# One transformer layer on one core: attention unrolled, row maxima sent in halves, routing of the first batch placed in groups 4 to 7

## The reference

```python
x = x + attention(layernorm(x))      # x: 2 batches x 1024 tokens x 128, 16 heads of width 8
x = x + ffn(layernorm(x))            # 8 experts, top 2, capacity 512
# attention
q, k = rotary(x @ Wq + bq), rotary(x @ Wk + bk);  v = x @ Wv + bv
att = softmax(causal((q @ k.T + bias(bucket(i - j))) / sqrt(8)))
y = (att @ v) @ Wp + bp
# ffn, on u = layernorm(x)
probs = softmax(u @ Wr);  w, e = top_k(probs, 2)
pos = running count of the expert's earlier tokens;  keep = pos < 512
buf[e, pos] = u
buf_out = (gelu(rms(buf) @ Wg) * (rms(buf) @ Wu)) @ Wd + buf
combined = u + sum(w * buf_out[e, pos]);  fout = gated net of width 64 on rms(u), + u
out = where(a token overflowed, fout, combined)
```

## Time and profile before

| | us |
|---|---|
| median of 3 runs | 473.86 (473.33 to 474.39) |
| the profiled execution's own time | 474.48 |
| its span, first to last instruction | 472.7 |

### The profile page before, as it was taken

How to read it: one execution, slowest core, us unless ns; L and a number is a source line. 1 busy time by engine, 2 the same in 40 slices (tenths; PEclk the granted TensorE clock), 3 DMA queues, 4 the chain that set the end, 5 groups by cost and what they waited for, 6 DMA issues and landing times.

```text
span 472.7 us, 8283 instructions
## 1 busy us (share of the span) xinstructions
PE 384.9 (81%) x2440; PEld 184.7 (39%) x2440; DVE 320.9 (68%) x702; ACT 212.4 (45%) x471; POOL 283.7 (60%) x229
## 2 busy tenths in 40 slices
PE   3297398699999999997999999986877495999910
PEld 0154143343444434433434444342434241566510
DVE  3989369687786786864877867749566780466614
ACT  1024212377676776763766776766442100233300
POOL 6637800096767858863967669677367384066660
PEclk9689879799999999998999999998898597799975
DMA  8196881650532893507106200053001012123118
GB/s 231 34 272 135 174 185 23 162 99 2 95 78 79 269 183 64 112 6 133 39 3 122 50 3 1 0 164 105 2 23 55 27 46 67 47 85 96 46 44 266
DMA packets 32560, 42.90 MB, mean 91 GB/s; under 512 B 6043, under 2 KB 26395, under 8 KB 31147
## 3 DMA queue, kind: packets, MB, share of 16 engines
q1 hardware_dynamic: 29334, 35.62, 32.2%
q0 software_dynamic: 2048, 4.11, 2.6%
q10 hardware_dynamic: 1136, 2.65, 1.7%
HBM read 27.61 MB, written 12.75 MB: 85 GB/s over the span
## 4 chain that ended last, share of the span: by engine, by line
PE 63%; DVE 15%; DMA 7%; issue 7%; POOL 5%; SPq 1%; ACT 1%; ACTq 0%; DVEq 0%; POOLq 0%
PE ps_av L922 15%; PE ps_st L898 14%; PE ps_slot L826 13%; PE ps_slot L830 6%; PE ps_st L1017 3%; PE ps_slot L1027 3%; POOL slots L608 2%; DVE neg_max L1181 2%; DMA b_grp<-b_all 2%; PE ps_st L1019 2%; PE ps_slot L941 1%; PE ps_av L1019 1%; DMA bcol<-in_L_attn_bk_dram 1%; PE ps_slot L865 1%; POOL parts L617 1%
## 5 line engine op out<-in xcount | busy, mean ns | idle before, releaser
L1181 DVE TENSOR_REDUCE neg_max<-ps_slot 128x1 f32<-128x640 f32 (+7 forms) x184 | 176.1, 990 | 50.4 <-PE ps_slot L830 48.9
L688 ACT ACTIVATE probs<-ps_st 128x512 f32<-128x512 f32 (+3 forms) x384 | 164.6, 495 | 90.3 <-PE ps_st L898 88.0
L593 POOL TENSOR_TENSOR probs<-probs,f_grp 128x1024 f32<-128x1024 f32 (+1 forms) x70 | 140.9, 2018 | 5.3
L826 PE MATMUL ps_slot<-k_stack,q_stack 128*128 128x512 bf16 (+3 forms) x384 | 103.9, 336 | 10.4 <-DMA b_grp<-b_all 4.1
L898 PE MATMUL ps_st<-q_stack,k_stack 128*128 128x512 bf16 (+3 forms) x384 | 100.1, 332 | 4.7 <-DMA q_stack<-max_rows 3.2
L589 POOL TENSOR_SCALAR_AFFINE_SELECT probs<-probs 128x512 f32<-128x512 f32 x63 | 40.0, 635 | 100.1 <-ACT probs L688 100.0
L922 PE MATMUL ps_av<-probs,v_grp 128*32 128x512 f32 (+3 forms) x768 | 82.5, 504 | 0.7 <-POOL probs L593 0.4
L830 PE MATMUL ps_slot<-b_grp,flip_b 128*128 128x256 bf16 (+1 forms) x288 | 69.9, 267 | 0.0
L898 PEld LDWEIGHTS ps_st<-q_stack,k_stack 128*128 128x128 bf16 x384 | 34.9, 98 | 66.7 <-ACT probs L688 47.2
L826 PEld LDWEIGHTS ps_slot<-k_stack,q_stack 128*128 128x128 bf16 x384 | 36.5, 100 | 48.4 <-DVE neg_max L1181 14.5
L617 POOL DMA_INDIRECT parts<-probs,e_tok x32 | 31.4, 983 | 31.0 <-DVE probs L1433 22.2
(11 more groups left out here) (156 smaller groups left out, 391.3 us busy)
## 6 DMA issues: line engine op xcount, KB each, us to landing
q_stack<-q_parts SPq DMA_DIRECT2D x24, 192.0 KB
f_grp<-f_all SPq DMA_DIRECT2D x6, 512.0 KB, 10.1
slots<-in_c_rows_dram SPq DMA_DIRECT2D x4, 528.0 KB, 5.9
probs<-slots SPq DMA_DIRECT2D x8, 264.0 KB, 2.7
f_all<-g_vec SPq DMA_DIRECT2D x1, 2048.0 KB, 11.3
k_stack<-k_parts SPq DMA_DIRECT2D x16, 128.0 KB
b_grp<-b_all SPq DMA_DIRECT2D x8, 256.0 KB
parts<-in_c_rows_dram SPq DMA_DIRECT2D x4, 512.0 KB, 10.0
```

Of the source, the lines that this page charges most:

```text
L593: pool.tensor_tensor(pr, pr, f_grp[:, fbuf, :, fo:fo + hi - lo], ALU.mult).then_inc(near_done, 1)
L688: act.activation(probs[:, u % PBUF, g, c0:512], ps_st[:, n % 3, c0:512], ACT.Exp, scale=SCALE).then_inc(exp_done, 1)
L826: pe.matmul(ps_slot[:, slot, o + lo:o + hi], q_stack[:, buf, g, t * P:(t + 1) * P], k_stack[:, buf, g, lo:hi], start=True, stop=(nlo >= nhi))
L1181: dve.tensor_reduce(neg_max[:, heads[0]:heads[-1] + 1, t], src, AX.X, ALU.max, negate=True).then_inc(slot_used, 1)
```

## The change

- The loops and steps go. A list `PLAN`, made when the program is built, gives every item of all 8 groups in one order, and each engine walks it. The scores and values are laid out first; the maxima units of group n+1 are spread by their matmul columns from row 8 of group n to row 8 of group n+1 (a row is one ST; a group has 48). Group 0: 12 (with the one due at once, 13) maxima units ahead of its first ST, the rest with FLIPs 2 to 7 among its rows 0 to 7.
- Maxima in halves: M comes twice for a group, directly behind maxima unit 6 (queries 0 to 511) and behind unit 22. The scores of the second half of the queries (row 16 on) wait for the second M alone. `M_AT = 58` is now `M_AT = [6, 22]`.
- SP: `put_max(n, 0)`, `load_stack(n + 2)` (nine DMAs, once the exponentials of group n-1 are done), `put_max(n, 1)`. The stacks are stored by halves of the tokens; group 0's halves are loaded apart, the first after quarter 0.
- Quarters 0, 1, 2 are projected, then maxima units 0 to 6, M, then quarter 3, FLIP 0 and 1. DVE's statistics of batch 1 stand behind the rotation of quarter 1. `keep_warm(8)` stands behind quarter 2.
- `b_grp`, `f_grp` and `v_grp` and their copies go: PE and POOL read `b_all`, `f_all` and `v_all`. `VW`, the columns of a head's values, is 9 and not 32. `f_all` is loaded in two parts.
- Tokens: batch 0's units stand in groups 4 and 5 (A0 in unit 54, E0 in unit 67 of 96); POOL sends 12 of its 16 rows between its products from unit 70 on. Batch 1 is two spans of 4 tiles: A2, B2 in group 7, C2 and D1 among the last values, the second span behind. F and G stand last.

```diff
-SPANS = [(0, TPB), (TPB, TT)]
+SPANS = [(0, TPB), (TPB, TPB + CH), (TPB + CH, TT)]
+TOKENS_AT = {54: [("A", 0)], 55: [("A", 1)], 57: [("B", 0)], 59: [("B", 1)], 62: [("C", 0)], 63: [("C", 1)],
+             64: [("D", 0)], 65: [("X", 0)], 67: [("E", 0)], 92: [("A", 2)], 93: [("B", 2)], 94: [("NEAR", 10)],
+             95: [("NEAR", 11)]}
+TOKENS_LAST = [("A", 3), ("E", 1), ("B", 3), ("C", 3), ("D", 2), ("X", 2), ("E", 2),
+               ("F", 0), ("F", 1), ("F", 2), ("F", 3), ("G", 0), ("G", 1), ("G", 2), ("G", 3)]
...
+    out = [("QK", 0), ("QK", 1), ("QK", 2)]
+    d = 0
+    for i, (items, cost) in enumerate(t_items):
+        while d < len(due) and due[d][0] <= before[i]:
+            out.append(due[d][1])
+            if due[d][1] == ("M", 0, 0):
+                out += [("QK", 3), ("FLIP", 0), ("FLIP", 1)]
+            if due[d][1][0:2] == ("S", 0) and due[d][1][2] >= len(SUNITS) - N_FLIP + 2:
+                out.append(("FLIP", due[d][1][2] - len(SUNITS) + N_FLIP))
+            d += 1
         out += items
+    av = [("AV", NG - 1, u) for u in range(NU - AV_LAG, NU)]
+    return out + [av[0], ("C", 2), av[1], ("D", 1), av[2], ("EVAC", NG - 1, 1), ("X", 1), ("Y", NG - 1, 1)]
...
+                elif kind == "M":
+                    pe.wait_ge(slot_used, k)
+                    pe.transpose(ps_slot[0:HG * MT, slot, 0:P],
+                                 neg_max[:, what[2], :, :].rearrange("p g t -> p (g t)"), ident).then_inc(slot_full, 1)
...
+            for n in range(1, NG):
+                put_max(n, 0)
...
+                if n + 2 < NG:
+                    load_stack(n + 2)
+                put_max(n, 1)
...
+                    near_product(n, u)
+                    if NU * n + u >= DISPATCH_FROM and sent < 2 * TPB and (NU * n + u) % 3:
+                        if sent == 0:
+                            pool.wait_ge(init_out, 16 * E_NUM // 2)
+                        dispatch(*rows[sent])
+                        sent += 1
```

More of the change, by code:

```diff
@@ new lines, in t_cost, with s_cost, transposed_items @@
+def t_cost(u):
+    return HG * (512 - first_col(*UNITS[u]))
+def s_cost(su):
+    t, heads = SUNITS[su]
+    return len(heads) * (t + 1) * P
+def transposed_items():
+    out = []
+    for n in range(NG):
+        for u in range(NU):
+            tile, back = (u - AV_LAG) % NU, (1 if u < AV_LAG else 0)
+            items = [("ST", n, u, g) for g in range(HG)]
+            av = []
+            if n >= back:
+                av = [("AV", n - back, tile)]
+                if tile in (CH - 1, NU - 1):
+                    av.append(("EVAC", n - back, int(tile == NU - 1)))
+            at = AV_AT[u]
+            rows = [[i] for i in items]
+            if at < HG:
+                rows[at] = av + rows[at]
+            else:
+                rows[HG - 1] += av
+            if u == Y_AT[1] and n:
+                rows[HG - 1].append(("Y", n - 1, 1))
+            if u == Y_AT[0]:
+                rows[HG - 1].append(("Y", n, 0))
+            rows[HG - 1] += TOKENS_AT.get(NU * n + u, [])
+            out += [(r, t_cost(u) / HG) for r in rows]
+    return out
@@ new lines, in _, with stack_rows, part_rows @@
+            load_tiles(b_all, r_vec, 0, H, toep_in)
+            load_tiles(f_all, g_vec, 0, HG, factors_in)
+            def stack_rows(stack, buf, row, n, halves):
+                return stack[row:row + n, buf, halves[0]:halves[-1] + 1, :, :].rearrange("p h g t -> p h (g t)")
+            def part_rows(parts, n, part, count, halves):
+                w = HG * CW
+                return bass.AP(tensor=parts, offset=((n * NM + halves[0]) * 3 + part) * D * w,
+                               ap=[[w, count * D], [3 * D * w, len(halves)], [1, w]])
@@ L482, in _ @@
[L482 to L491 removed]
+            put_max(0, 1)
+            load_stack(2)
+            for n in range(1, NG):
+                put_max(n, 0)
+                if n + 2 == NG // 2:
+                    for i in range(2):
+                        for j in range(2):
+                            sp.wait_ge(parts_out[i][j], 2 * PART_OUT)
+                if n + 2 < NG:
+                    load_stack(n + 2)
+                put_max(n, 1)
+                if n == 2:
@@ new lines, in _ @@
+            sent = 0
+            for n in range(NG):
+                for u in NEAR:
+                    if n == NG - 1 and u in LAST_NEAR:
+                        continue
+                    near_product(n, u)
[4 more added lines that the diff above has]
+                        sent += 1
@@ L612, in _ @@
+            for t, k in rows[sent:]:
+                dispatch(t, k)
             pool.wait_ge(zero_out, 16 * (B * T // CAP))
@@ L646, in _, with split @@
             copy_xnT(0)
-            for c in range(NCH):
+            def split(c):
+                if c == 0:
+                    copy_xnT(1)
                 for i in range(2):
```

740 lines of the change are left out of this document (342 added, 398 removed).

## The result

The changed kernel takes 517.83 us (median of 4 runs, 517.32 to 523.16) beside 474.12 for the kernel before (473.33 to 476.5, 4 runs): ratio 1.0925, interval 1.0881 to 1.0968. Slower was right; 488 was 30 us short, and 517.8 lies outside the range (479 to 496) and above every rival's case.

The account below looks back on a forecast made before the run. PE was taken to bound the loop's steps, so its stalls are paid in full. Six terms gave 363.1 to the last exponential, + 30.5 + 23 + 70.3 = 486.9 us span, 488 on the median's footing; range 479 to 496.

Parts of the forecast that it names:

- E0: Batch 0's token unit in unit 67 of 96: ends the 36.6 us stretch of DVE's token work; no PE standing named.
- Term 1: Start: first maxima unit at 57 us, row 8 of group 0 reached at 90, bounds 83 and 93.
- Term 2: Seven stretches of scores with the next group's maxima: PE's work unchanged, 7 x 30.7 = 214.9 us.
- Term 3: M directly behind its last maxima unit, groups 1 to 7: PE stands still 14 x 1.54 = 21.6 us.
- first rival: PE's stalls at M are absorbed, so the 21.6 us go: 464 us, chance 0.20.
- Term 4: Second rows of maxima behind a stack's loads, groups 1 to 5: 0.4 us a group, 2 in all, bounds 0 and 24.
- third rival: Rows of maxima wait out the whole stack, 4.9 us late in five groups: 510 us, 498 if half; chance 0.12.
- Term 5: Batch 0's tokens in groups 4 and 5: DVE's excess work and waits cost 14 us, bounds 6 and 21.
- fourth rival: DVE's token work grows beside POOL, each norm piece doubling again: +7 us, 495 us, chance 0.09.
- Term 6: Group 7 and tail: ACT bounds scores, 20.6 us; then 30.5 to last positions, 23 to experts, 70.3 for experts.
- all cases: 464 to 498: Whole kernel: the time range stated for the forecast and all rivals together, in us.

Follow-up runs that it names:

- The experiment in the old kernel: Kernel before, with M directly behind the last maxima unit of a step and not 8 items later: 487.71 us, ratio 1.0286.
- the later M: Changed kernel with second rows of maxima ahead of the stack's loads and 14 of 16 M one maxima unit later: 494.47 us, ratio 1.0415.
- after_sp: Changed kernel with the second row of maxima issued on SP's queue ahead of a stack's nine loads: 506.93 us, ratio 1.0662.
- the fill: Changed kernel with 16 warm-up matmuls added behind token unit B1 and 8 behind each of D0 and E0: 512.85 us, ratio 1.0789.
- after_newton0: Changed kernel without the three Newton rounds in batch 0's second norm: 520.95 us, ratio 1.0661, on a chip where the kernel before took 488.0.
- the trace without rows: Changed kernel with none of POOL's token rows between its products, all 32 following the last product: 515.34 us, ratio 1.0846.
- best3: Changed kernel with maxima rows ahead of loads, M one unit later, 18 warm-up matmuls, norm in pieces, other batch 0 tokens in group 7, tail filled: 487.79, 472.56 us.

## Why the prediction fell short

By the prediction's terms, from the trace (the forecast span was 486.9, the measured 516.1):

- **Term 1, start.** Row 8 of group 0 stands at M(0, 1): 91.1 for 90. The total is right, in part by luck: the maxima started at 55.0 for 57, and from there it took 36 us and not 33.
- **Term 2, the stretches.** Too small by 0.8 a group, 5.6 us. Terms 2 and 3 made a plain group 33.8; it is 34.60 with two M a group, and PE is busy 31.50 in it and not 30.70. The row that grew is the turned scores' (13.3 us for 12.4); why was not separated. The narrower values gave half a microsecond a group at most (96 matmuls in 10.0 us, before 100 in 10.9). Group 0's stretch is 2.0 shorter than a plain one (32.6), which the prediction did not have: it holds 80 value matmuls and not 96.
- **Term 3, M behind its unit.** The mechanism is right, the size a little high. M's idle time is 1.32 for 1.54, in 14 places of groups 1 to 7 (one of them, 4.03, also holds D0's block), so 18.5 for 21.6. The experiment in the old kernel shows the wait alone (1.69 at each M), and the later M takes most of it away. The first rival (464) is refuted by both.
- **Term 4, rows behind the loads.** Mis-sized: 2 forecast; 7.6 on PE's rows and 10.3 in the traces. The step that failed is "behind the loads it lands with them, near 9.5 to 10". The rows take 6.4 to 7.4 us from issue, near the 8.64 of the earlier trace rows that I kept as the bound. "It decides from 5.0 us of landing time on" was right: 6.37 gives a wait of 1.36, 7.43 one of 2.43. It is the third rival's mechanism at less than half its size (22).
- **Term 5, tokens in groups 4 and 5.** The step that failed most: 14 forecast, 28.5 measured. The amount on DVE was right (69.5 busy in both groups, 21.1 over two plain ones, for 23.7). What was wrong is "25.6 + 23.7 - 36.6 = 12.7 too much" as the whole price: it lets DVE fill all its idle time, and nothing is added to it for PE. Shown in its place: DVE stays idle 28.3 of 97.7 us (`after_sp`), while PE stands behind each block and hands over nothing; the one block that was shortened went into the time whole (1.75 for 1.75). The standing is 15.0 in all. So the 14 would have been about right for the standing alone; what the term left out is the lower clock behind each standing (6.6, by the fill), for which the prediction had no figure, and PE's own token matmuls, about 7, which it had only as the lower bound. The places of the standings were named rightly (7.67 for "5 to 9", 4.03 for 3), and E0's 3.73 was left out. The fourth rival's mechanism is there (2.20 us at L1088, and the 4.69 of L1264 in `after_newton0`), but for 2 us here, not for the bulk.
- **Term 6, group 7 and the tail.** Group 7 took 26.9 for 20.6. The step that failed is "without maxima ACT bounds the scores". 1.9 are POOL's rows of tokens (25.0 without). For the other 4.4 no run changes one engine alone, but the trace without rows shows that ACT was not the bound: in 368.1 to 393.1 ACT is busy 17.8, POOL 19.9 and PE 21.9 us, so PE's own work was already more than 20.6, and the chain passes from one to the other. Behind it the forecast held: positions 28.2 us after the last exponential for 30.5, the experts 21.4 after that for 23, straight behind the warm-up; 69.5 for 70.3.

Summed: +1.1 (start), +5.6 (plain groups), -2.0 (group 0's stretch), +8.3 (rows of maxima), +14.5 (tokens), +6.3 (group 7), -4.7 (tail and experts) = 29.1 of the 29.2 that the span was off.

The range had a fault of its own: "all cases: 464 to 498" leaves out the 510 that the third rival is priced at, and each case changes one or two terms. Here terms 2, 4, 5 and 6 were all too low at once.

As for the change itself: with its three new waits mended the unrolled kernel reaches 472.6 to 475.5, level with the kernel before or 0.6% under it. Its plain group is then still 1.8 us longer than the old step (32.49 for 30.70), about 12.5 us over seven. So about as much must be gained elsewhere (no loop turn, earlier start, no copies, the shorter warm-up); what each of these gives was not measured alone.

## What to carry to other kernels

When two engines hand units to each other through two slots, the second one's idle time is not free room. Price a block put between its units at its full length, small pieces spread far apart at about half, and add the first engine's own share of the new work and the clock that it loses while it stands. If that is too much, move the block to where no units are handed over (16 us instead of 28 here). Place an instruction that reads a reduction one unit behind it, not directly. On a queue, issue the small transfer that someone waits for ahead of the bulk loads that nobody waits for yet.

## What the hardware showed that I had not expected

- 4 KB of rows issued 1.9 us behind a stack's loads landed in 6.4 to 7.4 us. With the rows issued ahead of the loads (`after_sp`) the median of all rows is 1.7.
- Adding 32 matmuls whose result nobody reads shortened two groups by 6.6 us (clock 0.89 and 0.85 to 0.96 and 0.93) and the kernel by 5 us.
- Taking 4.3 us of instructions out of a DVE block shortened it by 1.75 us: the POOL product that had lengthened one of them (2.20 for 0.17) now lengthened the scalings behind (4.69 for 2.14).
- On one chip the kernel before took 488.0 us, not 475. It was not traced there, but `best3` was, there and on another chip: the two traces agree to 0.6 us up to M(7, 1) and differ by 15.5 us behind it, 10.3 of them before the experts, where PE and DVE stood 2 to 4.5 us in several places with no releaser that the trace names. What it is stays open.
